# Two 12-bit float32r parts in place of three bfloat16 parts for q, k and the row maxima of a fused RWKV block and attention

## The chip, the cores and the metric

The kernel runs on one core of one Trainium2 chip. The metric is the device time of one execution in microseconds. The engines are named as in the profile: PE is TensorE (PEld its weight loads), DVE is VectorE, ACT is ScalarE, POOL is GpSimd, SP is SyncE, which here only issues DMAs.

## The reference, cut to what matters

The input is `x` of shape (2, 1024, 128). Two branches work on its layer norm `xn`, and the output is their sum with `x`:

```python
x  = L0_attn_x                       # (B=2, T=1024, C=128)
xn = layernorm(x)
out = x + rwkv_block(xn) + attention(xn)

# rwkv_block: h = LN(xn); k, v = h @ w_tk, h @ w_tv; gate = sigmoid(h @ w_tr)
#             y = wkv(decay, first, k, v)        # a scan over the 1024 tokens
#             x1 = xn + gate * y; h2 = LN(x1)
#             x1 + sigmoid(h2 @ w_cr) * (relu(h2 @ w_ck)**2 @ w_cv)

# attention: W_eff of q, k, v, o = W + U diag(S * gates) V of the two best of 8 experts, one set for each batch
q, k, v = xn @ Wq, xn @ Wk, xn @ Wv            # 16 heads of 8 columns
attn = softmax(q_head @ k_head.T)              # 16 x 2 matrices of 1024 x 1024
out  = (attn @ v) @ Wo
```

## The kernel before, in words

The 32 heads (2 batches of 16) are taken as 16 pairs of two heads. For each pair, scores are made twice. First, a query's scores of all keys are made with queries on the output partitions, only to find the row maximum: these products are the "places" (`fill_place`, L1375), 32 of 128x512 for each pair, and DVE reduces each to one column (`read_place`, L1192). Second, scores are made with keys on the output partitions, minus the maximum (`scores`, L1477), ACT takes exp of them into `probs` (`exps`, L982), and `values` (L1489) multiplies them with v and a column of ones in float32, which gives the context and the denominator.

q and k have to keep their float32 precision to a large extent. A float32 number is split into three bfloat16 parts (`PARTS = 3`), each the rounding of what the last ones left. For the first chunks (batch 0) the split is made in PSUM: ACT or DVE writes a part (`part`, L842 and L1120), and PE takes it off the bank with a product by the negative identity (`take_part`, L1286). For batch 1 POOL does it (`split_late`, L613). The products of parts are laid on the contraction rows: each head has 64 rows of `q_main`/`k_main` with eight of the nine products of parts (`K_PARTS = (3, 3, 2)`) and 8 rows of `q_tail`/`k_tail` with the ninth, and rows 32 to 34 of the tail hold the three parts of the maximum against rows of ones. A head's rows lie at partition 0 or 64, so that the two heads of a pair run in two halves of the array at the same time. So a place is one product of 64 rows, and a score is a product of 64 rows and one of 35 rows, summed in PSUM. SP's DMAs spread the parts of a pair onto these rows three pairs ahead (`load_pair`, L425), the tails one pair ahead (`load_tails`, L435), and then the maxima (`place_max`, L442), which POOL has split (`split_max`, L626) and PE has turned (`turn_max`, L1391). The rows of pair 0 are made by products with `row_of` (`pair_rows`, L1360) and copied from PSUM.

The order of all work is written out by hand. There is an opening of 46 places (`OPENING`) among which PE fits the other products of the front part (`FILL_JOBS`), and then 128 steps (16 pairs x 8 key tiles). In each step PE runs two places, the two halves of `scores`, two places, `values` of the step before, and the step's products of the rwkv block, if there are any:

```python
        def one_step(p, step):            # PE, L1502
            for at in ahead:  fill_place(at)
            scores(p, s, step, 0)
            scores(p, s, step, 1)
            for at in behind: fill_place(at)
            values(p, s, step - 1)
            for at in jobs:   product(at)
```

Places and products share a ring of three PSUM banks (`ring`, L368): the place or product at position n waits until that at n - 3 has been read. The rwkv block runs in four quarters of 256 tokens, one started every 26 steps (`GAP`), with its products at fixed steps after the start (`PRODUCT_STEP`: mean 26, var 28, cr 35, ck0 to ck3 36 to 39, cv 42). At the start of a quarter POOL copies its k, gate, v and x into `quarter_in` (L659), and all later operations read these windows. The first of them is the scan on DVE (L1152), which waits for the copy of k.

Before the opening there is the front part: layer norm, the gate network of the experts, the effective weights. Between its small products PE runs `warm(n)` (L1242): n products of the 128x128 `neg_ident` with itself, whose results nobody reads.

## Time and profile before

| | |
|---|---|
| median of 3 runs | 446.24 us (446.19 to 446.74) |
| the profiled execution | 446.84 us, of which its span is 444.7 us |
| granted TensorE clock, mean | 0.992 of full speed |
| PE busy | 425.7 us (96%) |
| DVE busy | 382.4 us (86%) |
| ACT busy | 341.8 us (77%) |
| POOL busy | 191.5 us (43%) |
| DMA | 20.46 MB, 27.6% of 16 engines in the queue q1 |

Matmuls are pipelined, and their ends are modelled: a row of one matmul is its latency, and the pace of a stream is read from the starts. So "PE busy 96%" is not an array that is full for 96% of the time.

### The profile page before, as it was taken

What the parts mean: (1) busy time and instruction counts of PE and PEld (TensorE: products, weight loads), DVE (VectorE), ACT (ScalarE), POOL (GpSimd) and SP (SyncE); (2) the same over time, 40 slices, a digit from 0 to 9 for tenths busy, and PEclk for the clock granted to TensorE, in tenths of its full rate; (3) what the DMA queues carried; (4) which work ended last, traced back from release to release, by engine and by line L of the source; (5) the groups of instructions that cost most, each with busy time, mean ns of one, the idle gap of its engine ahead of it and who ended that gap; (6) DMA issues with size and microseconds to landing.
All of it is one profiled execution on the core that took longest, in us unless ns stands there. A gap on an engine that the chain in (4) does not pass through costs nothing.

```text
span 444.7 us, 8583 instructions
## 1 busy us (share of the span) xinstructions
PE 425.7 (96%) x3256; PEld 147.0 (33%) x3256; DVE 382.4 (86%) x657; ACT 341.8 (77%) x466; POOL 191.5 (43%) x271
## 2 busy tenths in 40 slices
PE   1989989999999999999999999999999999999997
PEld 1735222333332223332323233333323232322335
DVE  8469898999999998989999789999978998979182
ACT  3447837879887799868789878878986977898572
POOL 5038780854561443573352447416263620423200
PEclk9998998999999999999999999999999999999999
DMA  7004403050515150413232322423241322050311
GB/s 240 11 7 54 48 5 35 9 72 14 69 19 70 16 70 14 63 17 61 26 60 27 60 28 23 62 42 43 39 48 20 56 26 47 1 129 6 108 47 49
DMA packets 45797, 20.46 MB, mean 46 GB/s; under 512 B 36828, under 2 KB 37500, under 8 KB 45756
## 3 DMA queue, kind: packets, MB, share of 16 engines
q1 hardware_dynamic: 44630, 18.96, 27.6%
q10 hardware_dynamic: 1126, 0.95, 0.6%
q8 instruction: 26, 0.43, 0.4%
q14 instruction: 15, 0.12, 0.1%
HBM read 4.74 MB, written 4.98 MB: 22 GB/s over the span
## 4 chain that ended last, share of the span: by engine, by line
PE 87%; DVE 8%; ACT 3%; issue 1%; DMA 1%; DVEq 0%
PE banks L1497 27%; PE banks L1484 22%; PE banks L1387 18%; PE banks L1448 8%; DVE half_max L1198 5%; PE banks L1349 3%; ACT probs L985 2%; PE banks L1245 1%; PE banks L1427 1%; PE banks L1355 1%; PE banks L1284 1%; PE banks L1435 1%; PE banks L1341 1%; PE banks L1250 1%; DVE stats L1044 1%
## 5 line engine op out<-in xcount | busy, mean ns | idle before, releaser
L1198 DVE TENSOR_REDUCE half_max<-banks 128x1 f32<-128x512 f32 x512 | 318.4, 682 | 21.4 <-PE banks L1387 19.4
L985 ACT ACTIVATE probs<-banks 128x1024 f32<-128x1024 f32 x256 | 248.2, 1023 | 53.0 <-PE banks L1484 49.8
L1497 PE MATMUL banks<-probs,v_op 128*32 128x512 f32 x1024 | 136.7, 606 | 0.0
L1387 PE MATMUL banks<-k_main,q_main 64*128 64x512 bf16 x512 | 117.5, 387 | 5.5 <-DVE half_max L1198 3.2
L1484 PE MATMUL banks<-q_main,k_main 64*128 64x512 bf16 x512 | 100.2, 379 | 0.4 <-ACT probs L985 0.2
L1484 PE MATMUL banks<-q_tail,k_tail 35*128 35x512 bf16 x512 | 100.2, 379 | 0.0
L1387 PEld LDWEIGHTS banks<-k_main,q_main 64*128 64x128 bf16 x512 | 36.7, 93 | 150.6 <-DVE half_max L1198 131.4
L1484 PEld LDWEIGHTS banks<-q_tail,k_tail 35*128 35x128 bf16 x512 | 27.3, 95 | 26.5 <-issue 0.6
L1484 PEld LDWEIGHTS banks<-q_main,k_main 64*128 64x128 bf16 x512 | 26.6, 96 | 25.3 <-ACT probs L985 10.2
L1497 PEld LDWEIGHTS banks<-probs,v_op 128*32 128x32 f32 x1024 | 20.2, 108 | 32.0 <-issue 31.0
L731 POOL TENSOR_TENSOR work<-work 128x512 f32<-128x512 f32 x16 | 16.7, 1042 | 28.6 <-ACT work L974 28.6
L1448 PE MATMUL banks<-hT,mat_sb 128*32 128x512 f32 x160 | 20.9, 592 | 0.0
L726 POOL TENSOR_TENSOR hT<-hT,run 128x512 f32<-128x512 f32 x8 | 9.5, 1190 | 18.5 <-ACT hT L963 18.5
L633 POOL CAST max_op<-max_left 128x16 bf16<-128x16 f32 x16 | 3.2, 198 | 32.9 <-DVE max_left L1203 32.7
L665 POOL TENSOR_TENSOR work<-run 128x512 f32<-128x512 f32 x4 | 4.2, 1042 | 30.5 <-DVE run L1144 30.5
L739 POOL TENSOR_TENSOR RT<-hT,xn_tok 128x256 f32<-128x256 f32 x8 | 5.7, 740 | 21.7 <-DVE xn_tok L1167 21.7
L1448 PE MATMUL banks<-work,mat_sb 128*32 128x512 f32 x128 | 14.5, 592 | 0.0
L706 POOL TENSOR_TENSOR hT<-hT 128x512 f32<-128x512 f32 x4 | 4.2, 1043 | 21.8 <-DVE hT L1162 21.8
L1178 DVE RECIPROCAL parts<-parts 128x512 f32<-128x512 f32 (+1 forms) x4 | 13.4, 3339 | 0.0
L1250 PE MATMUL banks<-ident,xn_tok 128*128 128x128 f32 x16 | 4.3, 433 | 9.2 <-DVE xn_tok L1037 9.2
L974 ACT ACTIVATE work<-banks 128x512 f32<-128x512 f32 x16 | 9.6, 599 | 4.3 <-PE banks L1448 4.3
L1167 DVE TENSOR_TENSOR xn_tok<-banks,xn_tok 128x512 f32<-128x512 f32 x4 | 2.8, 691 | 10.7 <-PE banks L1448 10.7
(186 smaller groups left out, 423.5 us busy)
## 6 DMA issues: line engine op xcount, KB each, us to landing
ctx_dram<-ctx_sb SPq DMA_DIRECT2D x15, 256.0 KB, 2.0
q_main<-parts SPq DMA_DIRECT2D x60, 48.0 KB
k_main<-parts SPq DMA_DIRECT2D x60, 48.0 KB
mat_sb<-in_mats_dram SPq DMA_DIRECT2D x2, 768.0 KB, 5.0
v_op<-V SPq DMA_DIRECT2D x16, 64.0 KB, 3.8
parts<-ctx_dram SPq DMA_DIRECT2D x4, 256.0 KB, 4.1
q_main<-parts SPq DMA_DIRECT2D x30, 32.0 KB
k_main<-parts SPq DMA_DIRECT2D x30, 32.0 KB
```

The lines of the kernel that those rows point to most:

```text
L726: g.tensor_tensor(mix_in[i][:, :, :], mix_in[i][:, :, :], h2[:, :, 0:QT], ALU.add).then_inc(mixed, 1)
L731: g.tensor_tensor(kk[i][:, :, :], kk[i][:, :, :], kk[i][:, :, :], ALU.mult).then_inc(kk_ready, 1)
L974: a.activation(flat(kk[i]), ring_bank(ring.index(("job", f"ck{i}", q))), ACT.Relu).then_inc(relu_ready, 1)
L985: a.activation(probs[:, (2 * step + h) % 4, :, :], banks[:, 2 * h:2 * h + 2, :], ACT.Exp).then_inc(b_read, 1)
L1178: v.reciprocal(den_T[0:rows, n, :], den_T[0:rows, n, :]).then_inc(recip_ready, 1)
L1198: v.tensor_reduce(half_max[:, n % 2, u:u + 1], ring_bank(at), axis=AX.X, op=ALU.max).then_inc(a_read, 1)
L1250: last = nc.tensor.transpose(token_tiles(bank(n))[:, k, :], xn_tok[:, 4 * n + k, :], ident[:, :])
L1349: mm(dst, mat("t" + "kvr"[m % 3]), mix_slot[m], start=True, stop=True).then_inc(kvr_ps, 1)
L1387: mm(dst, q_main[HALF * e:HALF * (e + 1), s, P * c:P * c + P], k_main[HALF * e:HALF * (e + 1), s, CHUNK * h:CHUNK * h + CHUNK], start=True ...
L1448: last = mm(dst[g:g + 32, :], weights[:, g:g + 32], moving, start=start, stop=stop)
L1484: last = mm(bank(2 * h + e), k_rows[HALF * e:HALF * e + used, at, P * step:P * step + P], q_rows[HALF * e:HALF * e + used, at, CHUNK * h:C ...
L1497: last = mm(banks[g:g + 32, PV_BANK, :], v_op[:, s % 2, step, e, :], probs[:, (2 * step + h) % 4, e, :], start=(step == 0), stop=True, ski ...
```

## The change

q, k and the maxima are split into two parts instead of three. [...] Four products of parts of 8 rows make 32 rows (`MAX_ROW`), and the maximum's two parts stand in rows 32 and 33 of `q_main` itself, against ones in `k_main`. `q_tail` and `k_tail` are gone: a place is one product of 32 rows, a score is one product of 34 rows. The ones of slots 1 to 3 are spread once by two DMAs. `neg_ident`, and so `warm`, `take_part` and `turn_max`, work in float32r too. `take_part` runs 4 times instead of 8, `pair_rows` has 2 products instead of 3, `turn_max` one of 64 columns instead of three of 32. A pair costs SP 8 DMAs in `load_pair` instead of 12, none for tails instead of 4, 2 for maxima instead of 3.

`quarter_in` and its copies are gone: the quarters read `kept_k`, `kept_v`, `kept_gate` and `xnT` in place through `quarter(t, q)`, and write over `kept_k`. To make room, `ctx_sb` lies over `u_s`, `w_last` over two matrices of `mat_sb` (its memset moves behind `us_ready`), and the contexts that come back from DRAM go to `kept_v` and `kept_gate` (which wait for `x1_ready`).

```diff
-PARTS = 3
+PARTS = 2
 HALF = 64
-MAX_ROW = 32
+MAX_ROW = PARTS * PARTS * HD
-K_PARTS = (3, 3, 2)
...
-        neg_ident = sb("neg_ident", [P, P], BF16)
+        neg_ident = sb("neg_ident", [P, P])
...
-        parts = sb("parts", [P, 2, PARTS, CHUNKS, CHUNK], BF16)
+        parts = sb("parts", [P, 2, PARTS, CHUNKS, CHUNK])
-        q_main = sb("q_main", [P, SETS, T], BF16)
-        k_main = sb("k_main", [P, SETS, T], BF16)
-        q_tail = sb("q_tail", [P, 2, T], BF16)
-        k_tail = sb("k_tail", [P, 2, T], BF16)
-        quarter_in = sb("quarter_in", [P, CHUNKS, CHUNK])
+        q_main = sb("q_main", [P, SETS, T])
+        k_main = sb("k_main", [P, SETS, T])
...
+        def exact(t):
+
+            return t.bitcast(F32R)
...
+        def quarter(t, q):
+
+            return t[:, :, QT * q:QT * (q + 1)]
...
-                    for window, whole in ((k_q, k_of), (gate_q, gate_of), (v_q, v_of), (x_q, xnT[:, :, :])):
-                        g.tensor_copy(window[:, :, :], whole[:, :, bass.ds(q * QT, QT)]).then_inc(windows, 1)
...
                 for _ in range(times):
-                    mm(bank(7)[:, 0:P], neg_ident[:, :], neg_ident[:, :], start=True, stop=True)
+                    mm(bank(7)[:, 0:P], exact(neg_ident[:, :]), exact(neg_ident[:, :]), start=True, stop=True)
...
             take_part(1, 0)
             take_part(2, 0)
+            take_part(3, 0)
             expert_weights(2)
             expert_weights(3)
-            take_part(0, 1)
-            take_part(3, 0)
-            take_part(1, 1)
-            take_part(2, 1)
-            take_part(3, 1)
...
-                mm(dst, q_main[HALF * e:HALF * (e + 1), s, P * c:P * c + P],
-                   k_main[HALF * e:HALF * (e + 1), s, CHUNK * h:CHUNK * h + CHUNK],
+                mm(dst, exact(q_main[HALF * e:HALF * e + MAX_ROW, s, P * c:P * c + P]),
+                   exact(k_main[HALF * e:HALF * e + MAX_ROW, s, CHUNK * h:CHUNK * h + CHUNK]),
                    start=True, stop=True).then_inc(a_ready, 1)
...
-                for q_rows, k_rows, used in ((q_main, k_main, HALF), (q_tail, k_tail, MAX_ROW + PARTS)):
-                    for e in range(2):
-                        at = s if q_rows is q_main else s % 2
-                        last = mm(bank(2 * h + e), k_rows[HALF * e:HALF * e + used, at, P * step:P * step + P],
-                                  q_rows[HALF * e:HALF * e + used, at, CHUNK * h:CHUNK * h + CHUNK],
-                                  start=(q_rows is q_main), stop=(q_rows is q_tail))
+                for e in range(2):
+                    here = slice(HALF * e, HALF * e + MAX_ROW + PARTS)
+                    last = mm(bank(2 * h + e), exact(k_main[here, s, P * step:P * step + P]),
+                              exact(q_main[here, s, CHUNK * h:CHUNK * h + CHUNK]), start=True, stop=True)
                 last.then_inc(b_ready, 1)
```

## Rows read from the trace of the kernel before

**Rows 1.** The page: busy time, and the chain that ended last.
```profile
PE 425.7 (96%) x3256; PEld 147.0 (33%) x3256; DVE 382.4 (86%) x657; ACT 341.8 (77%) x466; POOL 191.5 (43%) x271
...
PE 87%; DVE 8%; ACT 3%; issue 1%; DMA 1%; DVEq 0%
```

**Rows 2.** Timeline of one plain step: start us, us, engine, line, operation, count.
```profile
199.74 6.85 DVE L1198 TENSOR_REDUCE half_max<-banks 128x1 f32<-128x512 f32 x11
...
201.42 0.38 PE L1484 MATMUL banks<-q_main,k_main 64*128 64x512 bf16 x2
...
201.64 0.38 PE L1484 MATMUL banks<-q_tail,k_tail 35*128 35x512 bf16 x2
...
202.29 0.46 PE L1387 MATMUL banks<-k_main,q_main 64*128 64x512 bf16 x2
...
202.68 1.07 PE L1497 MATMUL banks<-probs,v_op 128*32 128x512 f32 x8
...
203.68 0.10 PEld L1387 LDWEIGHTS banks<-k_main,q_main 64*128 64x128 bf16 x2 [0.84 <-DVE half_max L1198]
```

**Rows 3.** Windows, a step each: PE, PEld, DVE, ACT, POOL busy; clock; DMA share; GB/s.
```profile
215.12:218.77 3.65, 3.65 (x29) 1.01 (x29) 3.26 (x7) 2.24 (x4) 2.92 (x9) 1.00 0.12 19
...
221.30:224.65 3.35, 3.35 (x30) 1.01 (x29) 3.15 (x6) 2.63 (x4) 0.00 (x0) 1.00 0.18 30
...
232.65:235.14 2.49, 2.49 (x21) 0.75 (x20) 2.49 (x5) 2.49 (x4) 0.98 (x1) 1.00 0.46 46
...
246.98:250.32 3.34, 3.34 (x29) 1.01 (x28) 2.48 (x5) 3.05 (x5) 1.03 (x2) 1.00 0.45 49
250.32:253.67 3.35, 3.35 (x29) 1.01 (x29) 2.49 (x5) 3.35 (x6) 1.25 (x2) 1.00 0.42 102
253.67:257.02 3.35, 3.35 (x30) 1.01 (x29) 2.49 (x5) 2.54 (x4) 3.26 (x6) 1.00 0.44 52
...
261.99:268.29 6.30, 6.22 (x54) 1.79 (x53) 4.57 (x9) 2.93 (x5) 2.38 (x7) 1.00 0.03 5
```

**Rows 4.** The same windows, two product steps before the first quarter's mean.
```profile
92.44:95.98 3.54, 3.54 (x23) 1.05 (x22) 3.14 (x6) 2.53 (x4) 1.38 (x2) 1.00 0.51 116
...
113.25:116.93 3.68, 2.79 (x22) 0.76 (x21) 3.68 (x7) 3.68 (x6) 0.84 (x1) 1.00 0.46 101
```

**Rows 5.** Timeline after the last places, behind an output product.
```profile
421.67 0.39 PE L1484 MATMUL banks<-q_main,k_main 64*128 64x512 bf16 x2
...
422.31 3.91 ACT L985 ACTIVATE probs<-banks 128x1024 f32<-128x1024 f32 x4 [2.25 <-PE banks L1484]
```

**Rows 6.** Timeline of the front part, around the split and the first place.
```profile
15.72 3.59 PE L1245 MATMUL banks<-neg_ident 128*128 128x128 bf16 x32
...
17.87 0.27 DVE L1086 TENSOR_SCALAR gates_r<-gexp,gsum 2x128 f32<-2x128 f32 x1
...
28.91 2.76 PE L1365 MATMUL banks<-parts,quarter_in 16*128 16x512 bf16 x12
29.11 0.74 DVE L1124 TENSOR_SCALAR parts<-banks,col_sb 128x512 bf16<-128x512 f32 x1
...
31.71 0.69 DVE L1140 CAST q_main<-banks 128x512 bf16<-128x512 f32 x1 [0.60 <-PE banks L1365]
```

**Rows 7.** Timeline: weight loads of float32 passes of 512 columns.
```profile
22.38 0.19 PEld L1284 LDWEIGHTS banks<-xnT,w_eff 128*128 128x128 f32 x1 [0.24 <-issue]
22.81 0.19 PEld L1284 LDWEIGHTS banks<-xnT,w_eff 128*128 128x128 f32 x1 [0.24 <-issue]
```

**Rows 8.** Groups by line and form: float32 passes of 128 columns; busy, mean ns.
```profile
L1558 PE MATMUL banks<-w_last,work 128*128 128x128 f32 x16 | 1.9, 275 | 0.0
...
L1558 PEld LDWEIGHTS banks<-w_last,work 128*128 128x128 f32 x16 | 1.9, 192 | 0.0
```

**Rows 9.** Windows: the granted clock around the first places.
```profile
31.00:32.00 1.00, 0.67 (x4) 0.09 (x1) 0.40 (x2) 0.59 (x1) 0.00 (x0) 1.00 0.10 16
...
34.00:35.00 1.00, 1.00 (x6) 0.74 (x4) 0.95 (x2) 0.67 (x1) 0.00 (x0) 0.50 0.38 45
```

More of the change, by code:

```diff
@@ L581, in _ @@
             pool.wait_ge(us_ready, 8)
+            g.memset(w_last[:, :, :], 0.0).then_inc(zeros_ok, 1)
             for n in CHUNK_ORDER:
@@ L1364, in pair_rows @@
                 for i in range(PARTS):
-                    last = mm(bank(j), row_of[:, t, i, :], parts[0:2 * HD, t, i, n, :], start=(i == 0),
+                    last = mm(bank(j), exact(row_of[:, t, i, :]), exact(parts[:, t, i, n, :]), start=(i == 0),
                               stop=(i == PARTS - 1))
```

183 lines of the change are left out of this document (83 added, 100 removed).

## The prediction

> **What bounds the kernel now.** I read the page first. PE is busy for 96% and holds 87% of the chain that ended last, DVE is at 86% [rows 1]. That only says that PE and DVE are the candidates. So I went to the timeline of one plain step and then to the windows of all 128 steps.
>
> In the plain step the starts give PE's pace. A pair of products of 512 columns (the two heads, in two halves of the array) starts every 0.22 us: main at 201.42, tail at 201.64 and so on to the places at 202.29 [rows 2]. Six pair slots (two for places, four for scores) are 6 x 0.217 = 1.30 us, then 0.17 us pass between the last places' slot and `values` at 202.68, and `values` holds PE for 1.00 us, until the next place's weights at 203.68 [rows 2]. That is 2.47 us of a 2.49 us step. At the same time DVE's 11 reductions take 6.85 us without a gap, 0.62 us each, so four of them are 2.49 us [rows 2]. The step has two limits that fall together: PE at 2.47, DVE at 2.49. ACT's two exps are 1.95 us (3.91 for four [rows 5]), and less than the step.
>
> The windows then show where PE alone sets the time. Of the 114 steps that have places, about 76 take 2.49 to 2.61 us with DVE full (the row at 232.65). The other 38 hold a product of the rwkv block or a scan: 3.35 us with a product of 128x512 in four column groups, which is 2.49 + 0.86, while DVE has only 2.48 to 3.15 us of work, and 6.30 us for cv with DVE at 4.57 [rows 3]. After the places end, PE and ACT alternate.
>
> **The score products.** The change removes the tail product of every score: two pair slots a step, 2 x 0.217 = 0.43 us of PE. What is left has the same columns in another type. This trace has no float32r product, so its pace is the first unknown. The bound from below is the bfloat16 slot, 0.217 us for 512 columns [rows 2]. From above it is a pass of a float32 product: its two passes of 512 columns follow each other at 0.43 us [rows 7]. I take 0.217: a float32 product of 512 columns takes 2 x 0.43 = 0.86 us, four times the bfloat16 slot, as if four products of halves were made, and a float32r product has one product of one reduced value. The rows show the factor of four and not its cause, so the other bound stays as a rival. The Trainium skill's page "FP8 and Floating Point Precision" (section TensorE Precision Notes) says that a true float32 product is four passes and that a reduced-precision mode reads four bytes and truncates; by that rule a slot would be one pass, 0.217 us, and the factor of four in the rows agrees with it.
>
> Weight loads are the second unknown. A float32 load of 128 columns has a row of 0.19 us, and passes with such a load follow each other at 1.79 / 16 = 0.11 us [rows 8], so it hides under a slot of 0.217 us. That holds if the two heads' loads still run together, as they do now (0.10 us for two [rows 2]).
>
> **What a step gains.** PE's own time falls from 2.47 to 2.04 us. A plain step stays at DVE's 2.49: it gains nothing, because DVE's four reductions are untouched. A step with more work on PE gains at most 0.43 us, and not below what DVE or ACT have to do in it. By the windows of the second quarter, step minus the larger of DVE and ACT, at most 0.43: mean 0.39, var 0.20, two of ck0's kind 0.25 and 0.20, then 0.29, 0 (ACT is full with 3.35), 0.43, and cv 0.43 [rows 3], 2.2 us together. A step of 3.03 us in which DVE has a scan gains nothing. Three quarters give 3 x 2.2 = 6.6 us, the fourth, whose later products come after the places, 1.5 us. Before the first mean lie seven product steps like that at 92.44, six with 0.40 to 0.43 us to gain and one at 113.25 in which DVE is full [rows 4]: 2.5 us. The sum is 10.6 us.
>
> I take 1.0 us off, for the ring. After the change PE fills the last place early, and DVE then has at most three places in the banks, 3 x 0.62 = 1.87 us. PE needs 1.17 (gap and `values`) + 0.86 (product) + 0.39 (a place's latency [rows 2]) = 2.42 us until the next place is there. DVE idles for 0.55 us, and the step is 3.04 us instead of 2.92: 0.12 us in about nine steps that neither bound covers. So I count 9.6 us. The lower end is about 7 us, if the bank of a product waits for ACT's read in more of them. The upper end is 38 x 0.43 = 16.3 us, if queues carry all slack from plain steps into product steps.
>
> **After the places.** There 13 steps run without DVE's reductions. ACT's two exps take 1.95 us, PE's step 1.97, so plain steps gain nothing. Behind a cv or output product ACT has run dry and starts when the first half of the scores is there (from 421.67 to 422.31 [rows 5]). That half has one slot less, 0.22 us, and the half after it too. Four such places give 4 x 0.22 = 0.9 to 4 x 0.43 = 1.7 us; I take 1.3.
>
> **The split in the front part.** Eight `take_part` become four and twelve `pair_rows` products eight. Now DVE's last part runs from 29.11 to 29.85, the twelve products from 28.91 for 2.76 us, and DVE's copy of the last rows starts at 31.71 [rows 6]. Without the third parts, DVE ends its second parts at about 28.0 (the last part falls away, 0.74, the add of W_eff moves behind, and one product stands between), PE has the effective weights done at about 27.8, and eight products at 0.217 us with their latency are ready at 29.7. So everything from the first place on starts 2.0 us earlier. POOL's moved memset of `w_last` (0.3 us) and the two DMAs of ones lie under this: the operands that POOL makes next are read about 3 us after they are ready now, and slot 1 of `k_main` some 20 us after its loads. The opening itself then runs as before; its places keep their 0.217 us.
>
> **warm.** The 60 products of 128x128 change type too. 32 of them take 3.59 us, 0.11 each, and they end at 19.2, a microsecond after `gates_ready` (18.14) [rows 6]: they are on the path. A float32 pass of 128 columns, load included, has the same 0.11 us [rows 8], so I take nothing. From above a float32r product of 128 columns could cost what both passes of a float32 one do, 0.22 us: +0.11 us for each of the 32, of the 8 before and of the 16 after, 56 x 0.11 = 6 us.
>
> **The rest at nothing, with its cover.** The 16 copies into `quarter_in` leave POOL, which is busy for 43% [rows 1]; only the first of each quarter had a reader that waited, at the quarter's start, and its cover now is the step's slack of POOL. SP loses 9 of its 21 DMAs for a pair; what it feeds is needed a pair or more later, except the maxima, which arrive earlier for it. `split_max` loses two of four small POOL operations. The new waits (`late_split` before the first context copy, `x1_ready` before the contexts return) are met some steps before. Without their cover each costs under a microsecond.
>
> **Sum.** 2.0 + 9.6 + 1.3 = 12.9 us off the profiled 446.84 us, 433.9. That execution is 2.1 us over its span and 0.6 over the median, so against the median it is 433.3 us.
>
> **Rivals.** *warm slows* (chance 0.25). The mechanism above works, but float32r at 128 columns takes up to 0.22 us: 433.3 + 6 = 439.3 us. For it: nothing in the trace shows a one-pass product of four-byte data at 128 columns. Against: the same columns in float32 passes pace at 0.11.
>
> *Float32r at the pace of a float32 pass* (0.09), the one that ends slower. Four slots of 0.43 us and 1.17 us are 2.89 us a step against 2.47. Then PE bounds every step with places: 114 x 0.42 = 48 us, and about 4 us more for the places of the opening, less 2 from the split: 496 us. It decides from a slot of (2.49 - 1.17) / 4 = 0.33 us on, where PE passes DVE in the plain step. For it: 512 columns of four bytes take 0.43 us a pass [rows 7]. Against: the factor of four.
>
> *Weight loads no longer hidden* (0.05). If the two heads' loads ran one after the other at 0.19 us [rows 8] and not under the products, a slot would be 0.38 us, a step 4 x 0.38 + 1.17 = 2.69 us, 0.22 us over now: 446 + 114 x 0.22 - 2 = 469 us. The Trainium skill's page "TensorE: Matmul & The Clock Gate" (section Weight-path perf modes) says that the fast weight load is not used for float32, which speaks for this one; the rows, 0.10 us for two bfloat16 loads [rows 2] and 0.19 us for one in float32 [rows 8], agree with it.
>
> *Little reaches the end* (0.08). PE's slack is given back: ACT and the ring hold the product steps, and PE's short idle times lower the clock. After PE's pause from 31.7 the granted clock was 0.50 [rows 9]; such a stretch of 3.4 us costs up to 1.7 us. With two or three of them and half of the step gain it is 442 to 445 us.
>
> The forecast itself has 0.53. The range goes from 428 (the upper ends of the steps and of the tail, in part) to 441 (warm in full and some of the friction); 441 and below holds forecast and the first rival, 0.78, and a part of the last. This kernel's measurement can tell 0.2%, about 0.9 us. Faster by more than that: 0.53 + 0.25 + 0.07 = 0.85; within it 0.01; slower 0.14.
>
> **What would show it.** Plain steps stay at 2.49 us with DVE full and PE waiting 0.4 us for a bank; PE starts pairs every 0.22 us in float32r; product steps are near 3.0 us where DVE and ACT allow it, cv near 5.9; the first place starts near 30.7 us; the 32 warm products take 3.6 us. The prediction is wrong if a pair's slot is over 0.33 us, or if warm is over 7 us, or if plain steps fall below 2.49, which would mean that DVE's 0.62 us was not its own.

## Result: 502 us instead of 446, and the profile after

The changed kernel takes 501.6 us (median of 4 runs, 484.4 to 514.4), the kernel before 446.5 us beside it (446.2 to 447.0): a ratio of 1.090 (1.084 to 1.096). The prediction was 433.3 us with a range of 428 to 441. The executions of the changed kernel differ more than those of before, by the granted clock of TensorE (0.97 in the one profiled, of 484.4 us, 0.96 in the one of 488.8 us, 0.90 in the two of 514.4 us), and every ratio here takes only the executions within 1.5% of the kernel's fastest, so this one rests on the first two.

The page of the changed kernel, profiled execution: busy time, clock in 40 slices, the chain that ended last, and the groups that answer to [rows 1, 2, 6].

```profile
span 482.5 us, 7255 instructions
PE 464.9 (96%) x2704; PEld 186.3 (39%) x2704; DVE 380.9 (79%) x654; ACT 341.3 (71%) x454; POOL 168.3 (35%) x215
...
PEclk9999975699999999999999999999999999999999
...
PE 93%; DVE 3%; ACT 2%; DMA 1%; issue 0%
...
L1181 DVE TENSOR_REDUCE half_max<-banks 128x1 f32<-128x512 f32 x512 | 319.6, 684 | 53.3 <-PE banks L1365 53.3
...
L1228 PE MATMUL banks<-neg_ident 128*128 128x128 f32 x60 | 14.1, 419 | 0.0
```

DVE does the same 512 reductions in about the same busy time, but it now waits 53.3 us for the places; PE has 552 matmuls fewer and holds more of the chain, 93%. PE's weight loads are busy for 186 us, against 147 in [rows 1], although there are fewer.

The windows of both kernels, one row a stage: the front part up to the first place, the opening up to the first `values`, the first three steps, the next 111 steps, and what comes after the places. Columns: window, length, busy time of PE, PEld, DVE, ACT, POOL (instructions), granted clock, DMA share, GB/s. Before:

```profile
0.00:32.65 32.65, 21.26 (x120) 13.89 (x121) 20.91 (x81) 14.28 (x53) 10.31 (x31) 1.00 0.26 87
32.65:69.92 37.27, 34.58 (x131) 12.90 (x131) 33.12 (x54) 23.27 (x38) 26.86 (x31) 0.92 0.31 36
69.92:79.84 9.92, 9.92 (x66) 2.90 (x65) 8.36 (x14) 6.98 (x9) 1.39 (x2) 0.96 0.24 25
79.84:398.00 318.16, 316.35 (x2577) 100.10 (x2576) 295.45 (x488) 267.86 (x331) 146.01 (x198) 1.00 0.31 43
398.00:444.66 46.66, 43.59 (x366) 17.19 (x365) 24.54 (x23) 29.37 (x38) 6.97 (x11) 1.00 0.17 52
```

After:

```profile
0.00:37.87 37.87, 27.44 (x112) 22.41 (x113) 18.07 (x78) 12.03 (x41) 8.55 (x31) 1.00 0.23 76
37.87:80.08 42.21, 40.04 (x121) 16.57 (x121) 32.86 (x53) 23.18 (x38) 22.61 (x23) 0.84 0.27 31
80.08:96.08 16.00, 16.00 (x55) 4.61 (x53) 8.94 (x14) 7.23 (x9) 2.09 (x2) 0.57 0.11 10
96.08:437.12 341.04, 340.32 (x2106) 124.71 (x2105) 296.50 (x488) 269.99 (x331) 128.67 (x151) 1.00 0.28 37
437.12:482.53 45.41, 41.11 (x316) 17.96 (x315) 24.51 (x23) 28.89 (x38) 6.37 (x9) 1.00 0.15 50
```

The span grew by 37.87 us: front part +5.22, opening +4.94, first three steps +6.08, the 111 steps +22.88, the end -1.25. The largest term lies where the clock is 1.00 in both kernels, so there is a cost in every step that is not the clock's; the second and third terms go with clocks of 0.84 and 0.57.

The timeline of one plain step after, to be laid beside [rows 2]:

```profile
205.94 0.18 PEld L1365 LDWEIGHTS banks<-k_main,q_main 32*128 32x128 f32 x2 [0.84 <-DVE half_max L1181]
205.95 0.50 PE L1365 MATMUL banks<-k_main,q_main 32*128 32x512 f32 x2
...
206.37 0.73 PE L1460 MATMUL banks<-q_main,k_main 34*128 34x512 f32 x4
206.48 2.48 DVE L1181 TENSOR_REDUCE half_max<-banks 128x1 f32<-128x512 f32 x4 [0.22 <-PE banks L1365]
...
207.03 0.37 PEld L1365 LDWEIGHTS banks<-k_main,q_main 32*128 32x128 f32 x2 [0.37 <-issue]
...
207.65 1.07 PE L1472 MATMUL banks<-probs,v_op 128*32 128x512 f32 x8
...
208.65 0.18 PEld L1365 LDWEIGHTS banks<-k_main,q_main 32*128 32x128 f32 x2 [0.84 <-DVE half_max L1181]
```

The step is 2.70 us, not 2.49. One place alone has 0.50 us where it was 0.386 before, its weight load 0.18 where it was 0.10, and DVE now idles for 0.22 us of each step until the first place is there.

The individual starts behind these rows (worked out of both traces, instruction by instruction) give a loop that [rows 2] shows only if it is followed through the banks. Places use a ring of three banks, so the last place of a step waits for the bank of its first:

```
                                              before     after
first place -> last place of the step          1.173     1.278   (its latency 0.386 / 0.497, reduction 0.68, release)
last place -> values                           0.314     0.427
values -> first place of the next step         0.998     0.996
                                               2.49      2.70
```

The scores run beside DVE's reduction of the first place and are in no term of it. At two places of the loop the change adds 0.11 us, and that is what a weight load of 128 columns in float32r holds the array for: the experiments below bear this out. The load of the last place starts when DVE releases the bank (its reduction ends at 207.17 and the load starts at 207.22). The load of the first place starts only when `values` has streamed (at 208.65, though its bank has been free since 207.77).

### The profile page after: what moved, and what is told of

It reads as the page before. It is cut to its first block, busy times and chain, and to the rows that moved or that the text cites. A ratio compares the mean times of both kernels' runs of the same rounds, so it can differ in the third digit from the quotient of the medians.

```text
span 482.5 us, 7255 instructions
## 1 busy us (share of the span) xinstructions
PE 464.9 (96%) x2704; PEld 186.3 (39%) x2704; DVE 380.9 (79%) x654; ACT 341.3 (71%) x454; POOL 168.3 (35%) x215
## 4 chain that ended last, share of the span: by engine, by line
PE 93%; DVE 3%; ACT 2%; DMA 1%; issue 0%
PE banks L1365 28%; PE banks L1472 26%; PE banks L1460 18%; PE banks L1425 8%; PE banks L1328 3%; PE banks L1228 3%; ACT probs L970 2%; DVE half_max L1181 2%; PE banks L1404 1%; PE banks L1334 1%; PE banks L1412 1%; PE banks L1267 1%; PE banks L1320 1%; PE banks L1233 1%; DVE stats L1029 1%; PE banks L1372 1%
## 5 line engine op out<-in xcount | busy, mean ns | idle before, releaser
L1181 DVE TENSOR_REDUCE half_max<-banks 128x1 f32<-128x512 f32 x512 | 319.6, 684 | 53.3 <-PE banks L1365 53.3
L1365 PE MATMUL banks<-k_main,q_main 32*128 32x512 f32 x512 | 157.5, 507 | 3.7 <-DVE half_max L1181 1.8
L1472 PE MATMUL banks<-probs,v_op 128*32 128x512 f32 x1024 | 139.0, 615 | 0.2 <-ACT max_rows L889 0.2
L1365 PEld LDWEIGHTS banks<-k_main,q_main 32*128 32x128 f32 x512 | 70.1, 186 | 154.2 <-DVE half_max L1181 102.7
L1460 PE MATMUL banks<-q_main,k_main 34*128 34x512 f32 x512 | 97.3, 455 | 1.5 <-ACT probs L970 1.5
L1460 PEld LDWEIGHTS banks<-q_main,k_main 34*128 34x128 f32 x512 | 39.4, 188 | 40.4 <-ACT probs L970 21.5
L715 POOL TENSOR_TENSOR work<-work 128x512 f32<-128x512 f32 x16 | 16.7, 1041 | 32.5 <-ACT work L959 32.5
L624 POOL CAST max_op<-max_left 128x16 fp32r<-128x16 f32 x16 | 3.2, 197 | 38.7 <-DVE max_left L1186 38.7
L1228 PE MATMUL banks<-neg_ident 128*128 128x128 f32 x60 | 14.1, 419 | 0.0
L1161 DVE RECIPROCAL kept_gate<-kept_gate 128x512 f32<-128x512 f32 (+1 forms) x4 | 13.4, 3340 | 0.0
L1228 PEld LDWEIGHTS banks<-neg_ident 128*128 128x128 f32 x60 | 13.3, 328 | 0.3
L1328 PE MATMUL banks<-work,mat_sb 128*128 128x512 f32 x16 | 11.3, 796 | 0.0
```

Of the source, the lines that this page charges most:

```text
L715: g.tensor_tensor(kk[i][:, :, :], kk[i][:, :, :], kk[i][:, :, :], ALU.mult).then_inc(kk_ready, 1)
L1161: v.reciprocal(den_T[n][0:rows, :], den_T[n][0:rows, :]).then_inc(recip_ready, 1)
L1181: v.tensor_reduce(half_max[:, n % 2, u:u + 1], ring_bank(at), axis=AX.X, op=ALU.max).then_inc(a_read, 1)
L1228: mm(bank(7)[:, 0:P], exact(neg_ident[:, :]), exact(neg_ident[:, :]), start=True, stop=True)
L1328: mm(dst, mat("t" + "kvr"[m % 3]), mix_slot[m], start=True, stop=True).then_inc(kvr_ps, 1)
L1365: mm(dst, exact(q_main[HALF * e:HALF * e + MAX_ROW, s, P * c:P * c + P]), exact(k_main[HALF * e:HALF * e + MAX_ROW, s, CHUNK * h:CHUNK * h ...
```

## Experiments

Times are medians with the lowest and highest run; a ratio is to the kernel before on the same chip. The stages of each profiled execution stand in a table at the end.

**The places read bfloat16.** Only the places take the high halves of the same float32 tensors (32 rows), so the maxima are less exact.

```diff
+        def coarse(t):
+            return t.bitcast(BF16)[:, 1::2]
...
-                mm(dst, exact(q_main[HALF * e:HALF * e + MAX_ROW, s, P * c:P * c + P]),
+                mm(dst, coarse(q_main[HALF * e:HALF * e + MAX_ROW, s, P * c:P * c + P]),
...
```

> The changed kernel with one edit: the places read the high halves of the float32r values as bfloat16 (same bytes, same rows, same 32-row tiles); the row maximum comes out less exact, and a softmax doesn't depend on it. Theory A, the exposed weight load: a plain step is a loop from the first place of a step over its reduction (0.68 us), the release of its bank, the last place of the step, values (0.99) and the next step's first place, and a float32r weight load of 0.107 us stands open in it twice. Then the bfloat16 load gives both back: plain steps go from 2.70 to 2.49 us, product steps from 3.55 to 3.1 or less, the span from 482.5 to 450 to 458. Theory B, the tile sizes: places of 32 rows and scores of 34 rows (which take a 64-row tile) alternate, and each change empties the array. Then plain steps stay near 2.70. Theory C, the float32r products themselves are slow: plain steps fall by the share of the places, and the scores' spacing (0.33 us) doesn't move.

478.6 us (474.1 to 479.8), ratio 1.070 (1.064 to 1.076). A plain step is 2.50 us and a product step 3.36: nearly the whole 0.21 us is gone, with the scores still in float32r. Its timeline has for one place, to be laid beside the rows of the changed kernel (0.18 and 0.50 us):

```profile
202.88 0.10 PEld L1369 LDWEIGHTS banks<-k_main,q_main 32*128 32x128 bf16 x2 [0.84 <-DVE half_max L1185]
202.88 0.40 PE L1369 MATMUL banks<-k_main,q_main 32*128 32x512 bf16 x2
```

So the extra time of the steps sits in the places. This run changes their loads and their streams together; that it is the load, and not the float32r stream, is shown by the scores, whose float32r products of 512 columns follow each other after 0.24 us in the changed kernel with 64 rows (further down), and by the warm products of 32 columns below. The total stays high because of half-clock stretches (at 17.0, 61.3, 71.6 and 129.6 us, the last 37.5 us long).

**Places of 34 rows.** The rival to the load was the change of tile size between places (32 rows) and scores (34 rows, which take a tile of 64). Here two rows of zeros are put in, the maxima move behind them, and the places read 34 rows and the scores 36, so that both are tiles of 64.

```diff
+MAX_AT = MAX_ROW + 2
...
-                mm(dst, exact(q_main[HALF * e:HALF * e + MAX_ROW, s, P * c:P * c + P]),
...
+                mm(dst, exact(q_main[HALF * e:HALF * e + MAX_AT, s, P * c:P * c + P]),
...
-                    here = slice(HALF * e, HALF * e + MAX_ROW + PARTS)
+                    here = slice(HALF * e, HALF * e + MAX_AT + PARTS)
```

> The changed kernel with places of 34 rows in float32r (two rows of zeros added, the maxima moved to rows 34 and 35), so that places and scores use tiles of the same 64 rows. Theory A (exposed loads in the loop over values and the ring): the loads at the two ends of values stay open, plain steps stay at 2.65 to 2.70 us. Theory B (alternating tile sizes): plain steps return to 2.49 us and the span falls by 20 us or more. In both, the spacing from places to scores may shrink from 0.43 to about 0.32 or 0.22 us, because a load can run ahead again; only theory B says that this reaches the step.

489.8 us (483.1 to 528.2), ratio 1.088 (1.079 to 1.097). Plain steps stay at 2.70 us. From the first place to the scores it is 0.34 us instead of 0.43, so the change of tile does cost about 0.1 us there, but off the loop. The rival falls. The half-clock stretches are still there (17.1 us from 43.1 and 23.9 us from 73.8), so they do not come from places in tiles of 32 rows either.

**The kernel before without its main score product.** The prediction priced the removed product at 0.43 us in every product step. This kernel leaves the product of 64 rows out of every score (and so does not compute the scores) and changes nothing else.

```diff
-                for q_rows, k_rows, used in ((q_main, k_main, HALF), (q_tail, k_tail, MAX_ROW + PARTS)):
+                for q_rows, k_rows, used in ((q_tail, k_tail, MAX_ROW + PARTS),):
```

> The kernel before with one product of 35 rows for each score; it leaves out the scores' 64-row products (so the output is not the attention's). It is the saving that the prediction counted, by itself, in bfloat16. As predicted: plain steps stay at 2.49 us, product steps go from 3.35 to about 2.95, and the span from 444.7 to 432 to 436. If PE's time for scores lies off the path altogether, product steps stay at 3.35 and the span at 444. If PE is the bound everywhere, plain steps fall as well, to 2.1 us, and the span to about 400.

444.6 us (443.7 to 445.5), ratio 0.9945 (0.992 to 0.997). The stage rows of this kernel, steps and end:

```profile
81.19:399.30 318.11, 301.30 (x2133) 76.49 (x2132) 295.44 (x488) 267.17 (x331) 146.09 (x198) 1.00 0.31 43
399.30:443.27 43.97, 38.76 (x318) 15.79 (x317) 24.56 (x23) 28.67 (x38) 7.22 (x11) 1.00 0.17 54
```

PE has 444 matmuls less to do in the 111 steps, and they take 318.11 us against 318.16. Plain steps are 2.49 and product steps 3.35, as before. I had put 2.95 for product steps, and that was wrong: a product adds its 0.86 us to the loop (2.49 + 0.86), and the scores are off the loop there too. Only after the places, where the loop is gone, 2.69 us are won.

**The warm products in bfloat16.**

```diff
-                    mm(bank(7)[:, 0:P], exact(neg_ident[:, :]), exact(neg_ident[:, :]), start=True, stop=True)
+                    ones = neg_ident[:, 0:P // 2].bitcast(BF16)
+                    mm(bank(7)[:, 0:P], ones, ones, start=True, stop=True)
```

> The changed kernel with one edit: the 60 warm products read neg_ident as bfloat16 data instead of float32r (nobody reads their results). In the changed kernel they start every 0.213 us instead of 0.107, and the first product of the effective weights with x starts 7.2 us later than before. If the price is in the type of warm, the first place moves from 37.9 to about 30.7 us, two below the kernel before's 32.65, and the profiled span from 482.5 to about 475 or less; plain steps stay at 2.70 us. If the front part was late for another cause (the moved memset, the split), the first place stays above 35. The stretch at the half clock (66.5 to 93.8 us in the changed kernel) may move or shrink with it: that is open.

The first place starts at 30.89 us instead of 37.87, as expected. The timeline row of the 32 warm products, of the changed kernel and then of this one:

```profile
16.54 7.09 PE L1228 MATMUL banks<-neg_ident 128*128 128x128 f32 x32
```

```profile
15.83 3.60 PE L1229 MATMUL banks<-neg_ident 128*128 128x128 bf16 x32
```

The whole kernel takes 514.7 us (479.8 to 515.7). Its one execution with a clock of 0.96 took 479.8 us, 4.6 less than the fastest of the changed kernel; in the three others the clock is 0.88. In the profiled one of these (515.6 us) the 7 us of the front part were won and more was lost later, at half clock from 33.6 us (20.5 us long), 67.7 us (58.0 us) and 149.7 us (44.4 us).

**The warm products in float32r with 32 weight columns.** Same stream, a quarter of the load.

```diff
-                    mm(bank(7)[:, 0:P], exact(neg_ident[:, :]), exact(neg_ident[:, :]), start=True, stop=True)
+                    mm(bank(7)[0:32, 0:P], exact(neg_ident[:, 0:32]), exact(neg_ident[:, :]), start=True, stop=True)
```

> The changed kernel with warm products of 32 weight columns instead of 128, still float32r with 128 moving columns. It tells what the 0.213 us of a warm product are. If the weight load by columns sets them, they fall to 0.08 to 0.12 us; if 128 moving float32r columns stream at a quarter of the rate of 512, they stay at 0.21.

The timeline row of the 32 warm products of this kernel:

```profile
15.82 3.62 PE L1228 MATMUL banks<-neg_ident 128*32 128x128 f32 x32
```

The 32 products take 3.62 us, 0.11 each, against 0.22 with 128 weight columns. So the stream of 128 columns in float32r has the pace of bfloat16, and the rest is the load of the other columns. In the changed kernel the single starts show it standing open: a product at 20.017 us, the next load at 20.123, its product at 20.230, and so on in turn. (One execution, 515.6 us.)

**Everything in bfloat16**, still in two parts, so q, k and the maxima are less exact.

```diff
-            return t.bitcast(F32R)
+            return t
```

with `neg_ident`, `parts`, `q_main`, `k_main`, `max_op` and `max_rows` declared as bfloat16.

> The changed kernel with every float32r tensor of it made bfloat16 (two bfloat16 parts, so q and k are less exact); places of 32 rows, scores of 34 rows, order and semaphores as in the changed kernel. If the type is what costs, plain steps are 2.49 us, product steps 3.35 (the ring's loop holds them, as in the kernel before with half the score products), warm takes its old 0.107 us each, the first place comes at about 30.7 us, and the span is 439 to 443 us. The open question is TensorE's clock. If the long stretches at half clock in the float32r kernels come from the type, this kernel has a few of 3.4 us as the kernel before; if they come from fewer rows and fewer products in the array, it has stretches of 15 us and more too, and a span of 460 or more.

467.2 us (459.2 to 473.6), ratio 1.030 (1.024 to 1.035). Plain steps take 2.48 us, and the first place comes at 30.46. But the half-clock stretches are there too (10.2 us from 64.4, 37.5 us from 119.0), and the clock is 0.94. They do not need float32r.

**The kernel before with places of 32 rows.** It leaves out half of the products of parts in the maxima; the rest is the kernel before.

```diff
-                mm(dst, q_main[HALF * e:HALF * (e + 1), s, P * c:P * c + P],
+                mm(dst, q_main[HALF * e:HALF * e + 32, s, P * c:P * c + P],
...
```

> The kernel before with places of 32 rows instead of 64; it leaves out half of the products of parts in the row maxima, which only makes the maxima less exact. Tile sizes now alternate between 32 and 64 rows in bfloat16. Plain steps should stay at 2.49 to 2.50 us and the span at 444 to 446, if alternating tiles cost only PE time that is off the loop. If fewer rows lower the clock, long stretches at half clock appear here as well and the run is 10 us or more slower; if only the type does it, they don't.

469.0 us (465.3 to 470.1), ratio 1.048 (1.043 to 1.053).

Its windows (opening, first three steps, 111 steps):

```profile
32.21:77.03 44.82, 42.31 (x132) 15.06 (x132) 32.90 (x53) 22.95 (x37) 26.83 (x31) 0.73 0.25 29
77.03:86.98 9.95, 9.95 (x66) 2.56 (x65) 9.06 (x15) 7.52 (x10) 1.54 (x2) 1.00 0.31 30
86.98:416.41 329.43, 328.75 (x2579) 87.00 (x2577) 303.68 (x488) 268.89 (x331) 145.62 (x198) 1.00 0.30 41
```

Two things come from rows alone, with no float32r in the kernel. The opening takes 44.82 us at a clock of 0.73 instead of 37.27 at 0.92. And plain steps are 2.61 us instead of 2.49. The starts show where: from the first place to the first scores it is 0.32 us instead of 0.23, and to the last place, which here comes behind four score slots and a second change of tile, 1.30 instead of 1.17. So a change between tiles of 32 and 64 rows costs PE time, which reaches the step with four score slots in it (the kernels with two have 2.50 us).

**Both bfloat16 edits** (warm and places) in the changed kernel.

> The changed kernel with warm in bfloat16 and the places through their bfloat16 halves: scores, split and turns stay in float32r. At the full clock its terms add up to 482.5 less 7.2 (warm), 16 (27 us at half clock), 0.2 x 111 (steps) or about 439 us. With the clock as it was in the two kernels with one of these edits (0.92, 0.88) it comes to 470 to 500 us: then the clock is the larger part of what float32r costs here.

465.4 us (450.3 to 479.4). The first place comes at 30.38, plain steps take 2.50 and product steps 3.36 us, but 10.2 us from 35.8 and 23.9 us from 59.7 at half clock. The four executions line up with their clocks: 450.3 at 0.981, 457.6 at 0.963, 473.3 at 0.92, 479.4 at 0.904.

**More of the array at work, by extra products.** To the last kernel, products of 512 columns over all 128 rows that nobody reads: one ahead of the scores' second half in each step, also ahead of 16 places of the opening, or in the opening alone.

```diff
+            def stir(dst):
+                pe.wait_ge(rest_in, 16)
+                high = mat_sb[:, 16:20, :].rearrange("p m c -> p (m c)").bitcast(BF16)[:, 1::2]
+                mm(dst, coarse(mat("cv0")), high, start=True, stop=True)
...
+                if h == 1:
+                    stir(bank(2))
```

> This is the changed kernel with bfloat16 warm products and bfloat16 places (the high halves of the parts, so the maxima are less exact), and in each step one more product that nobody reads: a bfloat16 product of 512 columns over all 128 rows of the array, ahead of the scores' second half. Theory R (the granted clock falls because the pairs of products with 32 and 34 rows keep too little of PE's array at work): the half-clock stretch at 59.7 us of the kernel without the extra product (23.9 us) shortens where steps run, though the part of it that lies in the opening stays; plain steps stay near 2.50 us (PE has about 0.3 us open in one). Time about 452 to 458 us. Rival (the operands' type or the idle of PE lowers the clock, rows do not matter): the stretches stay as they are and the product adds its slot: 465 to 480 us.

513.3 us (509.0 to 515.6). Plain steps are 2.85 us: my "0.3 us open in PE" did not hold, since the product and the changes of tile around it move the second scores, and with them the last place, by 0.42 and 0.34 us. And 64.9 us from 59.5 are at half clock, with the extra product in every step. As I had put the theory, it fails here.

> As the kernel with the extra product in each step, and the same product also ahead of 16 of the opening's places. Theory R: half-clock stretches of 3.4 us at most, as in the kernel before; the first values start near 67.5 us (first place 30.4 us + the 37.3 us that the opening takes before), 114 plain and product steps take 328 to 336 us, and the tail 45.4 us: 443 to 450 us, which is at or a little below the kernel before. Rival (rows do not matter): stretches of 10 to 60 us stay, 465 to 480 us.

488.8 us (487.9 to 489.7). The opening, which had 0.71 before the extra products, runs at 0.98; but 10.2 us from 67.3, where the steps begin, are at half clock, and steps are 2.85 us. Neither range was met.

Its windows (opening, first three steps):

```profile
30.63:69.12 38.49, 37.91 (x139) 13.47 (x140) 33.73 (x53) 23.46 (x38) 22.61 (x23) 0.98 0.29 34
69.12:83.53 14.41, 14.41 (x58) 3.56 (x56) 9.15 (x15) 7.29 (x10) 1.77 (x2) 0.71 0.13 11
```

> The extra full-array products ahead of 16 places of the opening alone, none in the steps. Theory R: the opening takes 37 to 40 us instead of 47, and the stretches that start in the steps (as those at 119 and 129 us in other variants) can still come: 448 to 465 us, with more spread between executions than the kernel with the product in every step. Rival: no change of the opening, 465 us.

466.0 us (463.9 to 497.5). In the profiled execution, the one of 497.5 us, the opening takes 37.5 us at 0.98 instead of 44.6 at 0.71, as the theory had it, and then 41.0 us from 67.0 and 85.3 us from 131.8 are at half clock. So in the opening, products over all rows do hold the clock up. One of them among some twenty products of a step does not keep a stretch from starting, as the two kernels above show. Whether it shortens them is open: the 111 steps ran at 0.96 and 1.00 with it and at 0.85 without, one profile each.

**The 64 rows back.** Zeros are kept in the rows that 34 of 64 leave unused, and places and scores read all 64, with the same columns and the same number of products. In this kernel warm and places are bfloat16, and the diff is to the kernel with both of these edits. POOL clears the rows once, and two more DMAs a pair bring zeros over the old maxima.

```diff
-                mm(dst, coarse(q_main[HALF * e:HALF * e + MAX_ROW, s, P * c:P * c + P]),
+                mm(dst, coarse(q_main[HALF * e:HALF * (e + 1), s, P * c:P * c + P]),
...
-                    here = slice(HALF * e, HALF * e + MAX_ROW + PARTS)
+                    here = slice(HALF * e, HALF * (e + 1))
...
+            g.memset(q_main[:, 1:SETS - 1, :], 0.0).then_inc(cleared, 1)
+            g.memset(q_main[:, SETS - 1, CHUNK:], 0.0).then_inc(cleared, 1)
+            g.memset(k_main[:, 1:, :], 0.0).then_inc(cleared, 1)
```

> The changed kernel with bfloat16 warm products and places from the high halves (maxima less exact), and with zeros kept in the rows that 34 of 64 left unused, so that places and scores both read 64 rows of each head, as in the kernel before; POOL clears the rows in its free time of the front part, and each load of a pair brings two rows of zeros for the old maxima. Columns and slots are the same. Theory R (products over 32 or 34 rows keep too little of the array at work and the granted clock falls): half-clock stretches go back to some 3 us each; first values near 68 us (first place 30.4 + 37.3), steps 328 us, tail 45.3 us: 441 to 444 us, ratio 0.99 to the kernel before. Rival (rows do not matter, as the kernel with the extra full-array product in each step hints, whose stretch of 64.9 us came with it): stretches of 10 to 60 us stay, 455 to 475 us.

451.5 us (450.5 to 452.3), ratio 1.010 (1.008 to 1.013). Only 3.4 us in the opening and 2.7 us at the very end are at half clock: theory R holds for the clock. My total missed by about 8 us. About 4.8 lie in the steps (332.8 us for the 114, where I had put 328), 1.7 were won back in the opening, and 4.8 come from a cause which the timeline of DVE and POOL shows. In the kernel with both bfloat16 edits DVE's 12 operations took 3.15 us, here they take 7.48:

```profile
9.21 7.48 DVE L1034 TENSOR_SCALAR xn_tok<-x_sb,moments,rstd 128x128 f32<-128x128 f32 x12
```

```profile
10.45 1.80 POOL L582 MEMSET q_main<- 128x2048 f32 x1
12.19 0.52 POOL L583 MEMSET q_main<- 128x512 f32 x1
12.66 2.87 POOL L584 MEMSET k_main<- 128x3072 f32 x1
```

Four of the twelve operations have rows of 2.35 to 2.83 us instead of 0.34, and they end with the memsets: DVE stood while POOL cleared, and the first place came at 35.20 instead of 30.38 us. The Trainium skill's page "SBUF — State Buffer" (section Who interferes with whom) says that DVE in its two-port modes and GpSimd share one pair of ports, and that one of the two blocks wholly. These rows agree with it; that the twelve operations run in such a mode, no row shows.

**The same with 64 rows in the places alone.**

> The same, but the scores keep their 34 rows and only the places read 64. Theory R: the opening, which has no scores, takes 37 to 39 us as before; whether the steps hold the clock with 34 rows in the scores is what the run shows; 441 to 450 us if they do. Rival: as for the kernel with 64 rows everywhere, 455 to 475 us.

451.4 us (450.8 to 454.1), ratio 1.011 (1.007 to 1.015), with three stretches of 3.2 to 3.4 us. It is the rows of the places that count here; the scores can keep 34.

**The changed kernel itself with 64 rows**, float32r everywhere as in the change.

> The changed kernel as it is (float32r warm products and places) with 64 rows in places and scores and nothing else changed. Theory R: what the float32r weight loads cost stays (first place about 37.9 us, plain steps 2.70 us, 351 us for the 114 steps), and what the clock cost goes: opening near 38 us, tail 45.5 us, about 472 to 475 us instead of 482.5 (profiled) and 502 (median), with all executions close together. Rival: stretches stay, 482 to 515 us as for the changed kernel.

479.6 us (479.4 to 480.3), ratio 1.073 (1.070 to 1.076), with a clock of 0.996 and above in all four executions, where the changed kernel has 484 to 514 us.

Its windows, front part to the 111 steps:

```profile
0.00:42.50 42.50, 27.69 (x113) 22.59 (x114) 22.37 (x78) 12.03 (x41) 13.55 (x34) 1.00 0.21 68
42.50:80.31 37.81, 35.64 (x122) 15.70 (x122) 33.04 (x54) 22.88 (x37) 22.59 (x23) 0.97 0.30 35
80.31:91.12 10.81, 10.67 (x54) 3.67 (x53) 8.46 (x14) 7.70 (x11) 1.72 (x2) 0.94 0.21 19
91.12:432.49 341.37, 331.98 (x2105) 125.50 (x2105) 296.54 (x488) 270.20 (x332) 128.87 (x152) 1.00 0.28 38
```

These rows split the cost. The opening goes from 42.21 to 37.81 us and the first three steps from 16.00 to 10.81: 9.6 us of clock in the profiled execution. The 111 steps stay at 341 us: that is float32r. (The front part is 4.6 us longer for POOL's clearing.)

**The best version.** It has 64 rows, bfloat16 warm and places, and the zeros come from slot 0 by four DMAs instead of POOL.

```diff
+                here = slice(HALF * e + MAX_ROW, HALF * (e + 1))
+                for t in (k_main, q_main):
+                    sp.dma_start(t[here, 1:, :], t[here, 0:1, :].to_broadcast([HALF - MAX_ROW, SETS - 1, T])
...
```

> The kernel with 64 rows everywhere and bfloat16 warm products and places, but the unused rows are filled by four DMAs from slot 0 (whose unused rows are zero) and not by POOL; in the run before, POOL's memsets from 10 to 17 us held DVE's first eight operations and moved the first place from 30.4 to 35.2 us. My theory: the first place is back at 30.4 us, the opening takes 35.6 to 37.3 us (the kernel before takes 37.3), the 114 steps 333 us as measured, the tail 45.2 us: span 444 to 446 us, that is level with the kernel before, ratio 0.995 to 1.002. Rival: the 1.5 MB of zeros delay the loads of the second pair and its places, and the opening takes up to 42 us: span near 451 us.

446.4 us (445.9 to 447.7, 12 runs), ratio 1.0013 (1.0002 to 1.0023): level with the kernel before. Its maxima are less exact than those of both kernels compared. The first place is at 30.03 us. Its windows, opening to end:

```profile
30.03:68.49 38.46, 35.16 (x121) 12.35 (x122) 32.53 (x53) 22.84 (x37) 22.59 (x23) 0.91 0.46 72
68.49:78.12 9.63, 9.50 (x53) 2.81 (x52) 8.77 (x15) 7.44 (x10) 1.41 (x2) 1.00 0.27 23
78.12:400.42 322.30, 310.44 (x2106) 96.76 (x2105) 295.47 (x488) 268.41 (x331) 129.08 (x152) 1.00 0.29 40
400.42:445.56 45.14, 40.84 (x316) 17.88 (x315) 24.56 (x23) 28.72 (x38) 6.55 (x9) 1.00 0.15 50
```

2.6 us are won in the front part and 1.5 at the end, and 4.1 us are lost in the 111 steps: a step with the turn of the maxima takes 2.71 us instead of 2.53, and plain steps 2.51 instead of 2.49. The opening takes 38.46 us, more than the 35.6 to 37.3 that I had put, with 6.8 us at half clock from 55.5 us on. What makes the turn longer was not tried; with everything in bfloat16 it is still 2.66 us, against 2.48 for a plain step of that kernel.

The stages of the profiled executions in us (front part, opening, first 3 steps, 111 steps, end), the granted clock of the opening and of the first 3 steps, and the length of a plain step; "both" is the kernel with both bfloat16 edits:

| kernel | stages | clock | plain step |
|---|---|---|---|
| before | 32.65, 37.27, 9.92, 318.16, 46.66 | 0.92 / 0.96 | 2.49 |
| changed | 37.87, 42.21, 16.00, 341.04, 45.41 | 0.84 / 0.57 | 2.70 |
| warm bfloat16 | 30.89, 50.59, 17.39, 369.57, 45.43 | 0.66 / 0.50 | 2.70 |
| places bfloat16 | 36.06, 39.05, 15.33, 336.62, 45.32 | 0.87 / 0.56 | 2.50 |
| changed, places of 34 rows | 40.25, 48.67, 13.78, 341.30, 45.22 | 0.67 / 0.68 | 2.70 |
| all bfloat16 | 30.46, 37.29, 12.41, 333.03, 46.37 | 0.91 / 0.72 | 2.48 |
| both | 30.38, 44.56, 13.24, 322.08, 45.32 | 0.71 / 0.67 | 2.50 |
| before, places of 32 rows | 32.21, 44.82, 9.95, 329.43, 46.75 | 0.73 / 1.00 | 2.61 |
| both, 64 rows | 35.20, 35.60, 10.51, 322.32, 45.15 | 0.98 / 0.91 | 2.51 |
| both, 64 rows in places only | 35.28, 36.88, 10.79, 322.31, 47.11 | 0.95 / 0.84 | 2.51 |
| changed, 64 rows | 42.50, 37.81, 10.81, 341.37, 45.26 | 0.97 / 0.94 | 2.70 |
| both, 64 rows, DMAs | 30.03, 38.46, 9.63, 322.30, 45.14 | 0.91 / 1.00 | 2.51 |

## Why the prediction was wrong, step by step

The prediction went wrong in four of its terms: the weight loads of the places (taken as hidden, 24.3 us), the warm products (taken at nothing, 7.2 us), the score products (9.6 us of gain that did not come), and the granted clock (9.6 us in the profiled execution).

**"The step has two limits that fall together: PE at 2.47, DVE at 2.49."** Neither sum was the limit that mattered. The limit is the loop through the ring of three banks: first place, its reduction, last place, `values`, next first place. In [rows 2] the two sums agree with its 2.49 us to 0.02 us, which is why they looked like an explanation. And DVE's 0.62 us was not its own: in the same step its reductions start 0.60 us apart three times and 0.68 us apart once, where the next place has only just landed. Four of 0.60 are 2.4 us (an estimate from these starts), so DVE was held by the loop too.

**"A step with more work on PE gains at most 0.43 us", 9.6 us in all.** This step failed on the gain side. The scores run in the time in which the loop waits for DVE, in product steps too. The kernel before without its main score product measured it: 318.11 us against 318.16 for the 111 steps. The term is zero.

**The slot of float32r, 0.217 us.** Right for the stream: in the changed kernel with 64 rows the second scores follow the first after 0.24 us (0.22 in bfloat16), and 512 float32r score columns left the plain step at 2.50 us when only the places were changed. The rival of 0.43 us is refuted. In the changed kernel itself the second scores start 0.34 us after the first, with the first one's load in it. So the sign "a pair's slot is over 0.33 us" came, as did that of warm over 7 us (7.09), the first of them without costing anything in the loop.

**"It hides under a slot of 0.217 us."** This failed, and it cost most. It holds between two ready slots of 512 columns in tiles of one size. It does not hold for the two loads in the loop: that of the last place stands open behind DVE's release of the bank, and that of the first place behind `values`. That is two times 0.11 us a step, and 0.21 x 111 = 23 us. Places in bfloat16 gave it back (2.50 us a step), and tiles of one size did not (2.70). The rival *weight loads no longer hidden* had the right step length (2.69 against 2.70 us measured) by another mechanism, a load in every slot; it had a chance of 0.05. The Trainium skill's page "TensorE: Matmul & The Clock Gate" (section LDWEIGHTS) gives columns / 1.2 in ns for a load, which for 128 columns makes an estimate of 107 ns. The 0.107 us from a load of `warm` to its product (20.123 to 20.230) agree with it. Its section Weight-path perf modes leaves float32 out of the faster load and does not name float32r; rows of 0.18 us for a float32r load and 0.10 for a bfloat16 one agree, if float32r counts as float32.

**"Warm at nothing", "+0.11 us for each ... = 6 us" as the rival.** The rival, *warm slows* (0.25), was right, and a little small: the first product of `project` (the queries and keys, `xnT` with `w_eff`) begins 7.2 us later, and bfloat16 warm products gave 7.0 us back. 56 open loads are 6 us of it; the last microsecond was not followed. I had put 0.11 us a pass from [rows 8], where each load runs under the pass before it; the float32r loads of `warm` run between their products. Why these two differ was not tried.

**The front split, -2.0 us.** This was right: from the first product of `project` to the first place it is 8.76 us instead of 10.8. **After the places, -1.3 us.** Right: -1.25. **Copies, DMAs, new waits at nothing.** Nothing in the runs speaks against it, and none tried it alone.

**The clock.** The prediction allowed two or three stretches of 3.4 us, of the kind that [rows 9] show. It did not ask what a place of 32 rows instead of 64 does. Undone in the changed kernel itself, this brings back 9.6 us in the profiled execution, and the spread of 484 to 514 us shrinks to 479.4 to 480.3; and done alone in the kernel before it costs 7.5 us in the opening. The other executions of the changed kernel are up to 30 us longer still, at lower clocks; they were not profiled, so of the 17 us between the profiled one and the median no stage can be named.

The sum for the profiled execution: warm +7.2, weight loads in the steps +22.9 and +1.4 in the opening and first steps, clock +9.6, split -2.0, end -1.25: +37.85 of +37.87 us. It closes because its terms are differences of the same stages: the clock is what 64 rows gave back in the opening and the first steps, and the +1.4 is what is left there. Measured by an edit of their own are the step's 0.21 us, the warm products and the clock. The +1.4 is argued.

## What to carry to other kernels

When two engines' sums both equal the step, follow one buffer around its ring before believing either: work that runs beside another engine's part of the loop gains nothing when it is removed, and 0.1 us of latency inside the loop costs in every round. Here a float32r weight load was hidden under a ready slot of 512 columns, but not behind a wait, not behind `values`, and not between products of 128 columns. So price one load for each such place in the loop, also where the load of the old type costs little. When a change makes products thinner in rows, look at the granted clock, in several executions.

## What the runs showed of the hardware that I had not expected

- The granted clock goes with the rows of the products, at the same columns and the same count. With places of 32 or 34 rows for each of two heads, every kernel had stretches of 10 to 85 us at 0.50 (1.2 GHz) in the opening and the steps; with 64 rows, the kernel before and five others had only stretches of 3.4 or 6.8 us there. Before such a stretch PE was mostly busy (in the changed kernel, busy for 10.00 of the 10.00 us from 50 us on and for 5.28 of the 6.00 us from 60 us on; its clock is 0.50 from 66.5 us on). The rows that were added to the changed kernel hold zeros, and help nevertheless. It is not the tile size: places of 34 rows, in tiles of 64, have the long stretches too. Why the clock goes with rows stays open.
- A float32r weight load of 128 columns costs 0.11 us more than a bfloat16 one in the places where it is open, while float32r streams of 128 and 512 columns keep about the bfloat16 pace (0.11 and 0.24 us).
- A change between tiles of 32 and 64 rows costs about 0.1 us (from place to scores 0.43 against 0.34 us in float32r and 0.32 against 0.23 in bfloat16; 2.61 against 2.49 us for the step of before).
- POOL's memsets of 5.2 us held DVE's 12 operations, 3.15 us of work, until 16.7 us.
